# Adjacency loads of the first graph-attention layer: the upper half of the partitions issued by GpSimd instead of ScalarE

## The reference

```python
# layer 0 (in this text), h = x
src, dst = h @ a1, h @ a2
e = leaky_relu(src[:, None] + dst[None, :], 0.01)
attention = softmax(where(adj > 0, e, -9e15), axis=1)
x = layernorm(x + attention @ h)

# layer 1: the same with wh = x @ weight_w in place of h, plus a bias
wh = x @ weight_w
e = leaky_relu((wh @ a_src)[:, None] + (wh @ a_dst)[None, :], 0.01)
attention = softmax(where(adj > 0, e, -1e9), axis=1)
x = layernorm(x + attention @ wh + bias)
```

## Time and profile before

| | us |
|---|---|
| median of 3 runs | 512.47 |
| lowest and highest | 512.09 and 514.31 |
| the profiled execution | 512.94 |
| its span | 511.1 |

### The profile page before, as it was taken

One profiled execution on the slowest core, in us unless ns is written; L12 is line 12 of the kernel. 1 busy time (PEld: TensorE's weight loads), 2 busy tenths in 40 slices (PEclk: granted clock), 3 DMA queues, 4 the chain that ended last, 5 costly groups with the idle time before them and its releaser, 6 DMA issues.

```text
span 511.1 us, 11789 instructions
## 1 busy us (share of the span) xinstructions
PE 445.8 (87%) x4420; PEld 416.2 (81%) x4420; DVE 401.3 (78%) x712; ACT 397.5 (78%) x619; POOL 85.8 (17%) x68
## 2 busy tenths in 40 slices
PE   0799678979979798997969989999999999989891
PEld 0479668969978796997869869999999998989791
DVE  3679999889898998989887989775766657574854
ACT  2685279777998888789873749889898989898941
POOL 0002211415133051412403200000101010101010
PEclk9987978988999799898989859999999999999897
DMA  7999999999999999999953001102020111102000
GB/s 198 245 224 277 275 263 293 338 299 333 312 307 315 328 321 306 322 321 299 320 173 125 1 1 44 42 9 86 12 82 19 73 34 58 57 35 75 20 12 10
DMA packets 80294, 87.71 MB, mean 172 GB/s; under 512 B 7298, under 2 KB 76162, under 8 KB 80258
## 3 DMA queue, kind: packets, MB, share of 16 engines
q1 hardware_dynamic: 45602, 52.98, 36.3%
q10 hardware_dynamic: 34656, 34.21, 24.7%
HBM read 77.74 MB, written 9.44 MB: 171 GB/s over the span
## 4 chain that ended last, share of the span: by engine, by line
issue 50%; DVE 21%; DMA 21%; PE 3%; POOL 2%; SPq 1%; ACT 0%; POOLq 0%; ACTq 0%; DVEq 0%
DMA stage<-in_adj 19%; DVE narrow L791 5%; DVE turned L803 3%; PE acc L418 2%; DVE pos L817 2%; POOL small L968 2%; DMA xn<-in_x 2%; DVE num L861 1%; DVE num L854 1%; DVE red L847 1%; DVE kept L728 1%; DVE bn L866 1%; DVE kept L725 1%; DVE neg L820 1%; SPq L225 1%
## 5 line engine op out<-in xcount | busy, mean ns | idle before, releaser
L557 ACT ACTIVATE neg<-srow,dcol 128x512 int8 (+1 forms) x512 | 352.8, 878 | 11.7 <-issue 8.2
L418 PE MATMUL acc<-xy_old,pos 128*128 128x195 bf16 x1024 | 195.2, 260 | 26.3 <-POOL pos L979 22.1
L418 PE MATMUL acc<-xy_old,neg 128*128 128x195 bf16 x1024 | 195.0, 261 | 0.0
L418 PE MATMUL acc<-stage,pos 128*128 128x195 bf16 x1024 | 179.4, 249 | 4.8 <-DVE red L829 4.8
L418 PE MATMUL acc<-stage,neg 128*128 128x195 bf16 x1024 | 179.4, 249 | 0.0
L418 PEld LDWEIGHTS acc<-xy_old,pos 128*128 128x128 fp8e4 x1024 | 106.2, 104 | 34.8 <-issue 33.5
L418 PEld LDWEIGHTS acc<-stage,pos 128*128 128x128 fp8e4 x1024 | 101.2, 99 | 9.9 <-issue 9.7
L418 PEld LDWEIGHTS acc<-xy_old,neg 128*128 128x128 fp8e4 x1024 | 105.7, 103 | 1.4
L418 PEld LDWEIGHTS acc<-stage,neg 128*128 128x128 fp8e4 x1024 | 100.7, 98 | 0.2
L791 DVE TENSOR_SCALAR narrow<-stage 128x4096 uint8<-128x4096 int32 x32 | 74.0, 2314 | 17.7 <-DMA stage<-in_adj 16.9
L820 DVE TENSOR_TENSOR neg<-neg,kept 128x1024 uint32<-128x1024 uint32 x32 | 39.2, 1224 | 44.7 <-ACT neg L557 44.1
(11 more groups left out here) (117 smaller groups left out, 326.6 us busy)
## 6 DMA issues: line engine op xcount, KB each, us to landing
stage<-in_adj ACTq DMA_DIRECT2D x64, 512.0 KB, 9.1
stage<-in_adj SPq DMA_DIRECT2D x64, 512.0 KB, 9.4
spill<-turned SPq DMA_DIRECT2D x16, 512.0 KB, 8.1
turned<-spill SPq DMA_DIRECT2D x16, 512.0 KB, 3.9
out<-x1s SPq DMA_DIRECT2D x8, 128.0 KB, 1.9
xn<-in_x SPq DMA_DIRECT2D x1, 768.0 KB, 16.7
kept<-in_x SPq DMA_DIRECT2D x4, 128.0 KB, 3.8
kept<-in_x ACTq DMA_DIRECT2D x4, 128.0 KB, 4.6
```

Of the source, the lines that this page charges most:

```text
L418: last = nc.tensor.matmul(acc[:, r, c * XW:(c + 1) * XW], masks[c][:, t // BYTES, t % BYTES, r * P:(r + 1) * P], xy[layer][:, g * GT + t, ...
L557: last = nc.scalar.activation(o[:, t // BYTES, t % BYTES, :], srow[:, bass.ds((s % 2) * 512, 512)], ACT.Sign, bias=dcol[:, layer, col:col ...
```

## The change

ACT issues no adjacency loads any more. SP issues a = 0 and 1 as before (and the stores); GpSimd issues a = 2 and 3 of every granule (`POOL_ROWS`) and both parts of x's rows. The upper loads count up semaphores of their own (`pool_loaded`), on which `to_bytes` waits besides `loaded`. GpSimd's program is rewritten: first x's rows of the first part, both first granules, the rest of x's rows; then in each granule `load_next` stands ahead of a `positive`. Nothing else is computed, loaded or stored than before.

```diff
+        SP_ROWS = ((0, 0, Q), (1, 0, Q))
+        POOL_ROWS = ((2, 0, Q), (3, 0, Q))
...
-        def load(queue, quarters, s, g):
+        def load(queue, parts, s, g, done=loaded):
             rows = rows_of(adj, s, GR, Q)
-            for a in quarters:
+            for a, q0, q1 in parts:
                 c = g * (NA * JC) + a * JC
...
+                queue.dma_start(stage[Q * a + q0:Q * a + q1, g % SLOTS, :].rearrange("p (m j) -> p m j", j=JC),
+                                rows[q0:q1, :, c:c + JC]).then_inc(done[g % SLOTS], 16)
...
-            load_rows(sp, slice(0, RB))
-            load(sp, LOWER, 0, 0)
-            load_rows(sp, slice(RB, IB // 2))
-            load(sp, LOWER, 0, 1)
+            load(sp, SP_ROWS, 0, 0)
+            load(sp, SP_ROWS, 0, 1)
...
-            load(act, UPPER, 0, 0)
-
-            def load_next(s, g):
-                act.wait_ge(narrowed, s * NG + g + 1)
-                load(act, UPPER, s + (g + SLOTS) // NG, (g + SLOTS) % NG)
...
-                load(act, UPPER, 0, 1)
...
                     signs(0, s + 1, g)
-                    load_next(s + 1, g)
...
-                dve.wait_ge(loaded[g % SLOTS], 16 * NA * (s * (NG // SLOTS) + g // SLOTS + 1))
+                dve.wait_ge(loaded[g % SLOTS], 16 * LOADS * (s * (NG // SLOTS) + g // SLOTS + 1))
+                dve.wait_ge(pool_loaded[g % SLOTS], 16 * len(POOL_ROWS) * (s * (NG // SLOTS) + g // SLOTS + 1))
...
+            load_rows(pool, slice(0, RB))
+            for g in range(SLOTS):
+                load(pool, POOL_ROWS, 0, g, pool_loaded)
+            load_rows(pool, slice(RB, IB // 2))
+
+            def load_next(s, g):
+                pool.wait_ge(narrowed, s * NG + g + 1)
+                pool.sem_inc(pool_turn, 1)
+                load(pool, POOL_ROWS, s + (g + SLOTS) // NG, (g + SLOTS) % NG, pool_loaded)
...
             for g in range(NG - 1):
+                load_next(0, g)
                 positive(0, g)
-            positive(0, 3)
-            with pool.Fori(0, NS - 1) as s:
-                for g in range(NG - 1):
-                    positive(s + 1, g)
+            load_next(0, NG - 1)
+
+            def body0(s, last=False):
+                load_next(s + 1, 0)
+                positive(s, NG - 1)
+                for g in range(1, NG):
+                    if g < SLOTS or not last:
+                        load_next(s + 1, g)
+                    positive(s + 1, g - 1)
                 inverse_std(0, s)
-                positive(s + 1, 3)
```

More of the change, by code:

```diff
@@ L153, in gat_kernel @@
         loaded = [sem(f"loaded{g}") for g in range(SLOTS)]
+        pool_loaded = [sem(f"pool_loaded{g}") for g in range(SLOTS)]
         s_x = [sem(f"s_x{n}") for n in range(2)]
@@ L219, in row_at @@
             return bass.ds(s // 2 * (2 * RB) + s % 2 + 2 * r, 1)
-        def load(queue, quarters, s, g):
+        SP_ROWS = ((0, 0, Q), (1, 0, Q))
+        POOL_ROWS = ((2, 0, Q), (3, 0, Q))
+        LOADS = len(SP_ROWS)
+        LOWER, UPPER = (0, 1), (2, 3)
+        def load(queue, parts, s, g, done=loaded):
             rows = rows_of(adj, s, GR, Q)
-            for a in quarters:
+            for a, q0, q1 in parts:
                 c = g * (NA * JC) + a * JC
-                queue.dma_start(stage[Q * a:Q * a + Q, g % SLOTS, :].rearrange("p (m j) -> p m j", j=JC),
-                                rows[:, :, c:c + JC]).then_inc(loaded[g % SLOTS], 16)
-        LOWER, UPPER = (0, 1), (2, 3)
+                queue.dma_start(stage[Q * a + q0:Q * a + q1, g % SLOTS, :].rearrange("p (m j) -> p m j", j=JC),
+                                rows[q0:q1, :, c:c + JC]).then_inc(done[g % SLOTS], 16)
         def load_tiles(queue, quarters):
@@ L266, in _ @@
                 sp.wait_ge(narrowed, g - SLOTS + 1)
-                load(sp, LOWER, 0, g)
+                load(sp, SP_ROWS, 0, g)
             with sp.Fori(1, NS) as s:
@@ L271, in _ @@
                     sp.sem_inc(sp_turn, 1)
-                    load(sp, LOWER, s, g)
+                    load(sp, SP_ROWS, s, g)
                     if g < NG - KEEP:
@@ L596, in body0 @@
                 signs(0, s + 2, 0)
-                load_next(s + 2, 0)
                 if not first:
@@ L602, in _ @@
             tables0()
-            load_next(0, 0)
             for g in range(1, NG):
                 signs(0, 0, g)
-                load_next(0, g)
             row_factors(0)
             signs(0, 1, 0)
-            load_next(1, 0)
             body0(0, first=True)
@@ L616, in _ @@
                 signs(0, NS - 1, g)
-                if g + SLOTS < NG:
-                    load_next(NS - 1, g)
             copy_wh(NS - 3)
@@ L982, in _ @@
             for g in range(NG - 1):
+                load_next(0, g)
                 positive(0, g)
-            positive(0, 3)
-            with pool.Fori(0, NS - 1) as s:
-                for g in range(NG - 1):
-                    positive(s + 1, g)
+            load_next(0, NG - 1)
[6 more added lines that the diff above has]
+                    positive(s + 1, g - 1)
                 inverse_std(0, s)
-                positive(s + 1, 3)
+            with pool.Fori(0, NS - 2) as s:
+                body0(s)
+            body0(NS - 2, last=True)
+            positive(NS - 1, NG - 1)
             inverse_std(0, NS - 1)
```

## The result

The changed kernel takes 565.57 us (median of 4 runs, 564.48 to 566.44) against 513.18 us for the kernel before on the same chip: a ratio of 1.102 [1.098, 1.106], 52 us slower. The forecast was 514.1 with a range of 504 to 536, so the time lies far above it. Medians are of all executions; ratios, and differences in us, leave out those that took over 1.5% longer than the fastest of their kernel (one each in act4k, relay and relay_sp).

The account below looks back on a forecast made before the run. Layer 0 was taken to run at the pace of a ring of DVE's narrow and two load queues, DVE's own work just below. Start -1.35 and six turns +3.0 gave +1.65 on 512.47: 514.1 us, range 504 to 536.

Parts of the forecast that it names:

- a ring of narrow, two queues and a short wait: Layer 0: narrow on DVE frees a slot, two queues fill it, DVE waits 2.2 us a superblock.
- the one that ends last: Steady part of layer 0: SP's queue, with the spills, carries 26.26 MB against ACT's 21.10 and finishes each superblock later.
- the later start of the upper loads costs nothing: At each narrow, the upper queue has a 6 us lead, gone if the pair takes over about 4 us; cost 0.
- The equal shares: Load queues in layer 0: SP's and GpSimd's were assumed to split the rate as before, 171 GB/s each of 342.
- the third rival: Shares move towards GpSimd: superblock 32.4 us, 530 us; with 4096 B packets 39.7 us, some 70 us more; chance 0.12.
- The sign that was named, equal packets in both queues: Sign that the forecast is right: SP's and GpSimd's queues show equal packets where both run.
- The second rival: Shares move towards SP's queue, so DVE's waits shrink: faster, 498 to 508 us, chance 0.17.
- The pair on GpSimd: GpSimd issuing two load DMAs a granule: 2.0 us a pair, bounds 0.99 and 6.3.
- The first rival: A pair over 2.6 us makes `positive` meet a narrow, where GpSimd stands still: 520 to 533 us, chance 0.28.
- The start: First granules: DVE's 2.35 us wait goes, x's parts come 1.0 us later: -1.35 us, bounds -2.35 and +0.95.
- The turn of the superblock: Pair between `inverse_std` and `positive` of granule 3 delays PE: 0.5 us a superblock with the other pairs, six turns +3.0.
- ACT's freed issue time: ACT's 64 load DMAs go, some 4 us a superblock; DVE does not wait for ACT there, so worth nothing.

Follow-up runs that it names:

- act4k: Kernel before, only ACT's adjacency loads read as 4 pieces of 4 KB a partition in place of 16 of 1 KB: 553.63 us, 1.074.
- relay: Kernel before, each of ACT's two load DMAs waits for a small GpSimd fill, placed where the change has its DMAs: 551.21 us, 1.071.
- relay_sp: Kernel before, SP's two loads of each slot wait for the small GpSimd fills, ACT's pair goes at narrow's end: 543.12 us, 1.055.
- same_half: Kernel before, SP issues quarters 0 and 2, ACT 1 and 3, so both queues write the same half at once: 577.45 us, 1.125.
- gp_spill: Kernel before, GpSimd issues the 16 spills in place of SP, loads untouched: 515.89 us, 1.004.
- late_act: Kernel before, ACT's pair of loads waits for DVE's next transposes instead of narrow's end: 573.76 us, 1.119.
- sp4k: Changed kernel, only SP's adjacency loads read as 4 pieces of 4 KB a partition: 549.56 us, 1.072.
- step1k: Changed kernel, SP's pair waits until GpSimd has issued its first DMA of the slot, SP's pieces stay 1 KB: 559.78 us, 1.090.
- order: Changed kernel, GpSimd's `inverse_std` moved behind the pair of loads for the next superblock's first slot: 564.69 us, 1.100.
- step4k: Changed kernel, SP's pair waits for GpSimd's first DMA of the slot, and SP's loads have 4 KB pieces: 540.22 us, 1.050.
- order4k: The step4k kernel with GpSimd's `inverse_std` moved behind the next pair of loads: 534.01 us, 1.041 against the kernel before.
- relay_both: Kernel before, SP's and ACT's loads both wait for the same two small GpSimd fills, so both halves start late together: 523.97 us, 1.023.

## Why the prediction was wrong

**What bounds the kernel** was read rightly as a ring of narrow, two queues and a short wait, with DVE's own work just below it. What was missed is what held the ring's pace. Rows 3 were taken for a limit of the queues; same_half shows that it is one of the halves, 212 GB/s into one against 342 into both. So the overlap of the halves is worth more than a third of the rate, and DVE, which already waited 2.2 us a superblock, had no reserve for losing it. Nor was SP's queue "the one that ends last" because of its spills: gp_spill took them away and gained nothing.

**The step that failed** is "the later start of the upper loads costs nothing", with its cover of 6 us for the upper queue. Relay measures a start 0.8 us late at +36 us, late_act one of mostly 2.8 to 5.5 us at +61. The lead of 6 us was the difference of the bytes of a whole superblock, spills included. It is no lead in the single slot, where both halves have 1 MB, and the trace of the kernel before has none. In 98 to 248 us (KB each, median us to landing):

```profile
stage<-in_adj SPq DMA_DIRECT2D x40, 512.0 KB, 8.5
stage<-in_adj ACTq DMA_DIRECT2D x40, 512.0 KB, 9.0
```

The packets that close ACT's loads end at most some 1.2 us before the slot is complete, and mostly with it. With the upper half late, SP's runs alone at the start of a slot and the late half alone at its end. Nor does the loss begin where the pair "takes over about 4 us": at 0.8 us most of it is there.

**The equal shares failed as well**: the sum had the loads move as before, and that the shares shift towards GpSimd, the third rival with a chance of 0.12, is what happened. In the changed kernel this is the larger part: taking it away gives 15 us back (sp4k), taking the step away 5 (step1k), and act4k has it alone at +40. Turns by packets stood in rows 4, and the sentence on the Trainium skill ("DMA: Bandwidth & Descriptors", SWDGE vs HWDGE vs iDMA) gave packets of up to 4096 B; the trace agrees, with 3.6 KB a packet over the whole run (34.61 MB in 9504). Its price by that page, a superblock of 39.7 us, lies near the 38.2 measured; its other size, 32.4 us, is too small. In part the nearness is luck, since the 38.2 us hold the late start too; with the packets alone (act4k, reduces at 77.32 and 295.65) a superblock takes 36.4. The error was in the chance: the rule on turns was already shown by a row, only the size of a packet was open, and nothing in the trace spoke against a large one. That the changed kernel costs 53 us and not 70 is because six superblocks lose 8.0 us each, not 9.9, and the seventh turn only 1.8. The sign that was named, equal packets in both queues, came true (116 and 116) while the bytes stood at 3 to 1: it counted the wrong thing. **The second rival**, faster by a shift towards SP, went the other way.

**The pair on GpSimd** was sized at 2.0 us; it takes 1.35, inside the bounds of 0.99 and 6.3. **The first rival**, a long pair, did not come about, but its lock shows once. These are DVE and GpSimd of the changed kernel in time:

```profile
176.54 2.29 DVE L781 TENSOR_SCALAR narrow<-stage 128x4096 uint8<-128x4096 int32 x1 [1.65 <-DMA stage<-in_adj]
...
177.11 1.97 POOL L231 DMA_DIRECT2D stage<-in_adj  x1 [6.05 <-issue]
...
178.75 2.18 DVE L807 SCALAR_TENSOR_TENSOR pos<-neg,turned 128x512 uint32<-128x512 uint32 x1
...
179.09 1.27 POOL L979 TENSOR_TENSOR pos<-turned,neg 128x512 uint32<-128x512 uint32 x1
```

A DMA that falls into a narrow takes 1.97 us instead of 0.65 and ends at 179.08, 0.25 behind it. So the rule on the lock (the Trainium skill, "SBUF — State Buffer", Who interferes with whom) holds for these DMAs where DVE's narrow started first; but the pairs wait for narrow's end, so they seldom meet one. The other direction is not shown. DVE's next operation takes 2.18 us instead of 0.69, but it ends 0.56 us behind the `positive` that follows the DMA (179.09 to 180.36), and beside load DMAs alone the same operation takes 0.69 (at 209.22 with two of them). Sp4k and order show the same once each.

This DMA is the second of its pair: the first was issued at 170.42, and GpSimd then stood for 6.05 us without a wait that the profile shows. That slot gives the one wait that ended on GpSimd's half (4.5 us). Each run in which GpSimd issues the loads has at least one such hold inside a pair, of 2.5 to 6 us, between 150 and 180 us; its cause stays open.

**The start** was put at -1.35 us with +0.95 as its end. The wait of 2.35 us did go (no idle time stands before the narrow at 33.78). But DVE's first operation on x came 5.8 us later, against a bound of 3.3:

```profile
14.30 2.29 DVE L668 TENSOR_TENSOR kept<-kept 128x2048 f32<-128x2048 f32 x1 [12.21 <-DMA kept<-in_x]
```

The queues of the changed kernel between 8 and 12 us:

```profile
q0 software_dynamic: 148, 0.55, 65.4%
q10 hardware_dynamic: 215, 0.20, 27.0%
q1 hardware_dynamic: 179, 0.09, 14.7%
```

GpSimd's loads, not needed yet, take 0.55 of 0.85 MB, while the tiles of x that DVE waits for come in the two other queues. The bound had supposed full turns of equal size, the same mistake as above. That it is the bytes of GpSimd's loads that make the tiles late fits these rows; no run took it apart. Net, the second narrow stands at 33.78 instead of 31.00, +2.8 us, and the first reduce at +3.7.

**The turn of the superblock**, +0.5 us each, cannot be seen beside the waits for SP's half: order moves it and changes nothing that can be told. Where the other causes are taken out (step4k to order4k) the turns are worth 5 to 6 us, 0.8 each, near the size that was priced but by another path: the move brings only the pair of loads forward, not the `positive` and the products that the 0.5 us were worked out from. **ACT's freed issue time** was put at nothing, and nothing in any run speaks for a gain. The further semaphore wait has no run of its own.

## What to carry to other kernels

Before a load is moved to another engine's queue, ask with which transfer it shares the rate, how large both packets are, and whether both still start together; which engine is free to issue matters less: ACT's freed time brought nothing here. Where two transfers are fast only side by side, delaying the early one as well can be cheaper than leaving one of them behind (relay against relay_both). A busy share of the DMA engines near 1 is no sign that the rate is reached: look at GB/s, and at MB per packet for each queue.

## What the runs showed of the hardware

- The rate of loads into SBUF had a limit for each half of the partitions: 196 to 220 GB/s into one half, by one queue or by two (changed kernel at 230 to 232 us, same_half at 131 to 133 us), against 342 into both (rows 3).
- The queues take turns by packets also with GpSimd's: 116 against 116 in 2 us, with 3.6 and 1.1 KB each. Packets of ACT's queue follow the pieces in the same way: with 4 KB pieces 3.6 KB each (17.78 MB in 4883).
- A step of 0.8 us between the halves costs 1.2 us a slot (relay, 36 us over 30 slots), a common delay of 0.8 us 0.4 a slot (relay_both, 11 us). That the step costs more than its own length is measured; how it grows from slot to slot was not followed, and the account above, with the halves alone at both ends of a slot, was not shown to explain it in full.
- A load DMA of 512 pieces takes GpSimd 0.65 us. Its first of a pair is issued mostly 0.6 to 1.1 us behind the narrow that it waits for, ACT's 0.17 (median). One that fell into a narrow took 1.97 us.
